# Side work of a half step between its logits and its maxima, on three engines, in a four-layer convolution and attention kernel

## The chip, the cores and the metric

The kernel runs on one NeuronCore of one Trainium2 chip. It is written with an explicit instruction order for each engine and with semaphores between them: TensorE (PE) multiplies, VectorE (DVE) reduces and combines, ScalarE (ACT) evaluates functions, GpSimd (POOL) does three tiny operations an image, and SyncE issues the DMAs. The metric is device time in microseconds.

## The reference, cut to what matters

The input is x, 16 images of 256 channels by 32 by 32, fp32. Four layers follow each other:

```
L0: Q,K,V = 1x1 conv of x to 128 channels; per channel a 32x32 attention:
    attn = softmax(Q K^T), y = attn V; x = batchnorm(conv(y)) + x
L1: xn = group_norm(x, 32 groups); q,k,v of 8 heads, 32 channels each, t = 1024 positions
    logits = (q*s)^T (k*s)              (1024 x 1024 for each head and image)
    weight = softmax(logits); out = w_proj (v weight^T) + b; x = x + out
L2: xn = group_norm(x, 16 groups); k,v = kv_w xn + b
    q = softmax(k over channels)*s; k = softmax(k over positions)
    out = gelu(group_norm((k v^T)^T q)); x = xn + out_w out + b
L3: add bias; upsample by 2 (12 taps, both axes); leaky ReLU * sqrt 2; downsample by 2
```

Inputs and outputs are fp32; nothing is computed on the host beyond laying out weights.

## The kernel before

The attention of L1 is the main stream. An image has 32 steps: two groups of four heads, two halves of the 512 query positions, and eight tiles of 128 key positions (STEPS = UNITS * NT). A step has two half steps, called pairs in the code, one for each two of the four heads. So an image has 64 half steps, numbered 2 * n + pair, and the period of one image b is a loop over them. In a half step the engines do:

- L, logits (line 1097): TensorE multiplies two heads' keys and queries into PSUM banks 0 and 1, and ScalarE takes their exponentials, E (line 944), into prob. The next logits into a bank wait for the exponential two before.
- M, maxima (max_products, line 1112): TensorE computes, for the step ten steps ahead (m = n + NT + LEAD), two products of 128 queries by 512 keys into the three banks 2, 3, 5 in turn. VectorE takes their row maximum, R (max_steps, line 659), and ScalarE the exponential less that maximum with its sum over the row, U (sums, line 956), so that softmax's row factors are known before the weights are computed. Product k waits for the sum k - 3: the second product of a half step therefore waits for the first sum of the half step before.
- V, values (line 1141): only in the half step with pair 0, that is the even ones. TensorE multiplies the weights of the step before with v, for four heads, into bank 4.
- S, side work: a list of small named tasks of all other layers. The table SIDE (line 53) gives each half step its names. A name can stand for work of TensorE, ScalarE, VectorE, SyncE and GpSimd at once, each engine walking the same table in its own program. Names of image b finish its own L1 projections (q1, k1, v1), of image i = b - 1 they do the projection, L2 and L3 (proj, kv, qT, o2, z, wu, hu, hd, wd), and of image j = b + 1 they do L0 and the start of L1 (l0, corr, av, wr, q0, k0, v0). Side products use PSUM banks 6 and 7; bank_free (line 1155) gives for each name the wait that frees its bank. "turn1" to "turn4" pass row factors of softmax between VectorE and TensorE.

TensorE has no side work in the half steps 0, 4, 10, 20, 23, 24, 26 and 43. In 18, 30, 32 and 36 it is short. Names used further on: q1a to k1b are halves of projections which ScalarE evicts (hi, line 991) and VectorE finishes (lo, line 648); v1a and v1b follow in 6 and 7; kv0 to kv7 are evicted by two additions of VectorE (lines 719, 720); proj0a to proj1b by line 710; wr0a to wr1b by line 640; qT0a to qT1b by a copy (line 771); corr0 and corr1 (line 1636) are 64 small products each in half step 21, followed by softmax work on VectorE and ScalarE (soft0a, soft0b, ksub0, ksub1, soft1, qe1, kexp0, kexp1), and ctx0a, ctx0b (line 1701) in 22 need kexp0 and kexp1; norm1a, norm2a, norm3a average statistics (line 1094). In L3, wu and hu (lines 1733, 1743) are the upsampling products, evicted by a VectorE transpose (line 789) and by ScalarE's Prelu into u (line 1027); hd and wd (lines 1751, 1760) downsample, evicted by transposes (lines 797, 804).

The order inside a half step before the change is:

```
TensorE: L  M  V(even)  S
ScalarE: E  U  S
VectorE: R  (normalise, every 16th)  S
```

SyncE and GpSimd walk the table alone. Before the first period, first() does the side work that image 0 needs and its first ten steps of maxima; after the last one, last(i) does the remaining names of image 15 in the order TAIL.

Of the kernel before, what the change touches and what calls it, by code (L numbers as in the profile page):

```python
# [107 lines left out]
def beside(n, i, j):  # L108

    for name in SIDE.get(n, ()):  # L110
        if name == "copy_x" or name.startswith(OF_B) or (i is not None and not name.startswith(OF_J)) \
                or (j is not None and name.startswith(OF_J)):
            yield name
# [17 lines left out]
def chain_kernel(nc, x, weights, vectors, rows, filters, consts, recd, out):  # L131
    with ExitStack() as ctx:
# [223 lines left out]
        def turn_at(n):  # L356


            return (n - 1) // NT + 1 if n % NT == NT - LEAD else None
# [142 lines left out]
        def _(dve):  # L502
# [156 lines left out]
            def max_steps(b, m, pair):  # L659

                k = 4 * (2 * (m % 2) + pair) + m % NT // 2
                for e in range(2):
                    at = Q4 * m + 2 * pair + e
                    dve.wait_ge(max_mm.sem, max_mm(b, at + 1))
                    dve.tensor_reduce(mxh[:, k, e:e + 1], ps[:, max_bank(b, at), :], AX_X, ALU.max,  # L665
                                      negate=True).then_inc(max_ok.sem, 1)
# [244 lines left out]
            def period(b, i, j):  # L911
                for n in range(STEPS):
                    t = turn_at(n)
                    if t is not None:
                        if t < UNITS or j is not None:
                            maxima_joined(b, t)
                    for pair in range(2):
                        m = n + NT + LEAD
                        if m < STEPS:
                            max_steps(b, m, pair)  # L920
                        elif j is not None:
                            max_steps(j, m - STEPS, pair)

                        of, u = (b, n // NT - 1) if n else (i, UNITS - 1)
                        if n % NT == 0 and pair == 0 and of is not None:
                            normalise(of, u)
                        for name in beside(2 * n + pair, i, j):
                            side(name, b, i, j)

            def last(i):  # L930
                normalise(i, UNITS - 1)
                for name in TAIL:
                    side(name, None, i, None)

            periods(first, period, last)

        @block.scalar
        def _(act):
# [27 lines left out]
            def halves(b, t):  # L966

                act.wait_ge(join_v.sem, join_v(b, 2 * t + 2))
                act.activation(apart[:, :, :], apart[:, :, :], ACT.Exp).then_inc(apart_ok.sem, 1)
# [82 lines left out]
            def period(b, i, j):  # L1052
                for n in range(STEPS):
                    for pair in range(2):
                        exponentials(b, i, n, pair)
                        t = turn_at(n)
                        if t is not None and pair == 0 and (t < UNITS or j is not None):
                            halves(b, t)
                        m = n + NT + LEAD
                        if m < STEPS:  # L1060
                            sums(b, m, pair)
                        elif j is not None:
                            sums(j, m - STEPS, pair)
                        for name in beside(2 * n + pair, i, j):
                            side(name, b, i, j)

            def last(i):
                for name in TAIL:
# [5 lines left out]
        def _(pe):  # L1074
# [22 lines left out]
            def logits(b, n, pair, i):  # L1097

                u, s = n // NT, n % NT
                for h in (2 * pair, 2 * pair + 1):  # L1100
                    k = Q4 * n + h

                    if k >= 2:
                        pe.wait_ge(p_ok.sem, p_ok(b, k - 1))
                    elif i is not None:
                        pe.wait_ge(p_ok.sem, p_ok(i, STEPS * Q4 + k - 1))
                    if s == 0 and h == 0:
                        pe.wait_ge(row_in.sem, row_in(b, u + 1))
                    pe.matmul(ps[:, k % 2, :], ks[0:STACK + 1, (u // 2) * Q4 + h, s * P:(s + 1) * P],  # L1109
                              qs[0:STACK + 1, u, h, :], start=True, stop=True).then_inc(s_mm.sem, 1)  # L1110
# [724 lines left out]
            def period(b, i, j):  # L1835
                for n in range(STEPS):
                    for pair in range(2):
                        logits(b, n, pair, i)
                        m = n + NT + LEAD
                        if m < STEPS:  # L1840
                            max_products(b, m, pair)
                        elif j is not None:
                            max_products(j, m - STEPS, pair, b)
                        if pair == 0 and (n or i is not None):
                            of, before = (b, n - 1) if n else (i, STEPS - 1)
                            values(of, before, i)
                        for name in beside(2 * n + pair, i, j):
                            side(name, b, i, j)

            def last(i):  # L1850
                values(i, STEPS - 1)
# [69 lines left out]
```

## Time and profile before

| | |
|---|---|
| median of three runs | 3770.84 us (3764.8 to 3772.77) |
| the profiled execution's own time | 3771.88 us |
| its span, first to last instruction | 3769.7 us |
| TensorE busy | 3572.7 us, 95% |
| ScalarE busy | 2968.4 us, 79% |
| VectorE busy | 2739.3 us, 73% |
| mean granted TensorE clock | 0.971 |

All times are of one execution taken by the hardware profiler. A row of the timeline gives a start and a duration in us, the engine, the line of the kernel, the operation with what it writes and reads, and how many such instructions are merged (x2); in brackets stands the time that the engine sat idle before and what ended it. An fp32 matrix product appears as two MATMUL instructions. Matmuls overlap in the records, so that starts tell more than durations. Image 7 lies from 1649.21 to 1872.21 us, and image 6 ends where it begins.

### The profile page before, as it was taken

How to read it: one execution, taken by the hardware profiler on the slowest of the kernel's cores; microseconds unless marked ns; L12 is line 12 of the kernel's file. 1: busy time of each engine (PE TensorE's matmuls, PEld its weight loads, DVE VectorE, ACT ScalarE, POOL GpSimd, SP SyncE). 2: the span in 40 equal slices, each digit the busy share in tenths (PEclk: the TensorE clock that was granted, in tenths of full speed). 3: DMA queues.
4: the chain of work that ended last, by engine and by line, in shares of the span. 5: the costliest groups of instructions: out<-in, count | busy, mean ns of one | idle time of the engine just before them, and what ended most of it. 6: DMA issues, size and time to landing. Idle time of an engine off the chain costs nothing.

```text
span 3769.7 us, 60230 instructions
## 1 busy us (share of the span) xinstructions
PE 3572.7 (95%) x22401; PEld 1773.8 (47%) x22401; DVE 2739.3 (73%) x4891; ACT 2968.4 (79%) x6992; POOL 41.4 (1%) x57
## 2 busy tenths in 40 slices
PE   6999999999999999999999999999999999999987
PEld 3445545354453545545354454545545354454423
DVE  5667778677777877778677787867778677787645
ACT  2888888888788887888878788887878878788852
POOL 0000000000000000000000000000000000000000
PEclk7889999999999999999999999999999999999998
DMA  2212120121211112120121211112120121211000
GB/s 78 60 40 63 41 71 7 51 60 40 73 38 37 44 43 68 40 71 12 48 58 46 68 38 46 34 44 67 41 72 13 48 56 46 68 38 48 21 17 12
DMA packets 75523, 175.79 MB, mean 47 GB/s; under 512 B 16352, under 2 KB 19040, under 8 KB 73184
## 3 DMA queue, kind: packets, MB, share of 16 engines
q1 hardware_dynamic: 74512, 170.69, 16.6%
q8 instruction: 178, 2.92, 0.3%
q10 hardware_dynamic: 720, 1.26, 0.1%
q14 instruction: 113, 0.93, 0.1%
HBM read 36.62 MB, written 17.30 MB: 14 GB/s over the span
## 4 chain that ended last, share of the span: by engine, by line
PE 80%; ACT 10%; DVE 6%; issue 3%; DMA 0%; SPq 0%; ACTq 0%; POOL 0%; DVEq 0%; POOLq 0%
PE ps L1081 30%; PE ps L1150 12%; PE ps L1109 11%; PE ps L1129 10%; ACT ps L963 5%; PE ps L1701 3%; PE ps L1751 3%; ACT u L1027 2%; ACT prob L954 2%; PE ps L1733 2%; PE ps L1636 2%; PE ps L1648 2%; PE ps L1760 2%; DVE mxh L665 1%; PE ps L1743 1%
## 5 line engine op out<-in xcount | busy, mean ns | idle before, releaser
L665 DVE TENSOR_REDUCE mxh<-ps 128x1 f32<-128x512 f32 x2048 | 1306.9, 679 | 297.9 <-PE ps L1129 291.4
L963 ACT ACTIVATE ps<-ps,mxh 128x512 f32<-128x512 f32 x2048 | 1371.1, 679 | 155.0 <-DVE mxh L665 132.4
L954 ACT ACTIVATE prob<-ps 128x512 f32<-128x512 f32 x2048 | 1124.7, 613 | 316.9 <-PE ps L1109 309.8
L1109 PE MATMUL ps<-qs,ks 97*128 97x512 f32 x2048 | 880.7, 507 | 10.6 <-ACT prob L954 10.5
L1129 PE MATMUL ps<-ks,qs 96*128 96x512 f32 x2048 | 690.6, 413 | 23.9 <-ACT ps L963 15.7
L1109 PEld LDWEIGHTS ps<-qs,ks 97*128 97x128 f32 x2048 | 348.6, 192 | 560.2 <-issue 297.5
L1150 PE MATMUL ps<-prob,vo 128*32 128x512 f32 x4096 | 566.2, 626 | 0.2 <-ACT prob L954 0.2
L1129 PEld LDWEIGHTS ps<-ks,qs 96*128 96x128 f32 x2048 | 396.1, 194 | 166.2 <-ACT ps L963 61.5
L963 ACT ACTIVATION_READ_ACCUMULATOR ps<-ps,mxh 128x1 f32 x2048 | 454.3, 222 | 0.0
L1081 PE MATMUL ps<-xn,wqk 128*128 128x512 f32 x512 | 246.2, 614 | 13.3 <-DVE lo L648 9.3
L1081 PE MATMUL ps<-wkv,xn 128*128 128x512 f32 x512 | 245.0, 608 | 3.7 <-DVE xn L592 3.7
L1081 PE MATMUL ps<-xb,wq 128*128 128x512 f32 x384 | 182.4, 606 | 9.1 <-SPq L440 7.5
L648 DVE SCALAR_TENSOR_TENSOR lo<-ps,vec,hi 128x512 fp32r<-128x512 f32 x128 | 95.9, 749 | 129.5 <-ACT hi L991 129.5
L797 DVE STREAM_TRANSPOSE k<-ps 128x512 f32<-128x512 f32 x128 | 133.2, 1079 | 74.5 <-PE ps L1751 74.5
L1743 PE MATMUL ps<-qe,up_m 64*128 64x512 f32 x512 | 143.6, 638 | 33.6 <-DVE qe L789 12.2
L1150 PEld LDWEIGHTS ps<-prob,vo 128*32 128x32 f32 x4096 | 81.8, 109 | 182.6 <-issue 178.9
L991 ACT ACTIVATE hi<-ps,vec 128x512 fp32r<-128x512 f32 x128 | 88.5, 691 | 95.1 <-PE ps L1081 95.0
L1081 PEld LDWEIGHTS ps<-xn,wqk 128*128 128x128 f32 x512 | 93.9, 193 | 142.8 <-issue 121.9
L1751 PE MATMUL ps<-u,dn_m 128*64 128x512 f32 x512 | 130.5, 611 | 28.4 <-ACT u L1027 23.9
L1027 ACT ACTIVATE u<-ps 128x1024 f32<-128x1024 f32 x128 | 134.8, 1056 | 26.8 <-PE ps L1743 26.8
L1081 PEld LDWEIGHTS ps<-wkv,xn 128*128 128x128 f32 x512 | 92.8, 191 | 122.0 <-issue 110.9
L1701 PE MATMUL ps<-v,k 128*128 128x257 f32 x512 | 134.5, 414 | 4.3 <-ACT k L1014 4.3
(120 smaller groups left out, 3434.2 us busy)
## 6 DMA issues: line engine op xcount, KB each, us to landing
qs<-hi SPq DMA_DIRECT2D x256, 128.0 KB, 2.4
ks<-hi SPq DMA_DIRECT2D x252, 128.0 KB, 2.3
xb<-in_x SPq DMA_DIRECT2D x32, 512.0 KB, 4.4
qs<-lo SPq DMA_DIRECT2D x128, 128.0 KB, 2.4
xa<-xb SPq DMA_DIRECT2D x16, 1024.0 KB, 4.7
recs<-recd SPq DMA_DIRECT2D x64, 256.0 KB
out<-xn SPq DMA_DIRECT2D x32, 512.0 KB, 2.6
ks<-lo SPq DMA_DIRECT2D x126, 128.0 KB, 2.3
```

The source lines that it names most:

```text
L665: dve.tensor_reduce(mxh[:, k, e:e + 1], ps[:, max_bank(b, at), :], AX_X, ALU.max, negate=True).then_inc(max_ok.sem, 1)
L797: dve.transpose(d1[:, p, :].rearrange("p (h c) -> p c h", h=H)[:, 16 * half:16 * half + 16, :], ps[:, bank_of(f"hd{ct}{half}{'ab'[p]}", i) ...
L954: act.activation(prob[:, n % 2, h, :], ps[:, k % 2, :], ACT.Exp).then_inc(p_ok.sem, 1)
L963: act.activation(ps[:, bank, :], ps[:, bank, :], ACT.Exp, bias=mxh[:, k, e:e + 1], accum_out=sumh[:, m // NT % 2, k, e:e + 1]).then_inc(su ...
L1027: act.activation(u2[:, q // 2, q % 2, :, :].rearrange("p a n -> p (a n)"), both(bank_of(name, i)), ACT.Prelu, alpha=SLOPE).then_inc(u2_in. ...
L1081: ins = pe.matmul(dst, lhsT, rhs, start=(n == 0), stop=(n == len(pairs) - 1))
L1109: pe.matmul(ps[:, k % 2, :], ks[0:STACK + 1, (u // 2) * Q4 + h, s * P:(s + 1) * P], qs[0:STACK + 1, u, h, :], start=True, stop=True).then_ ...
L1129: pe.matmul(ps[:, max_bank(b, k), :], qs[0:STACK, u, head, (s // 2) * P:(s // 2 + 1) * P], ks[0:STACK, (u // 2) * Q4 + head, e * HALF:(e + ...
L1150: ins = pe.matmul(ps[DH * h:DH * h + DH, 4, :], vo[:, s, (u // 2) * Q4 + h, :], prob[:, n % 2, h, :], start=(s == 0), stop=(s == NT - 1))
L1701: ins = pe.matmul(ps[:, bank_of(f"ctx{ct}", i), 0:C + 1], k2[:, t, ct * P:(ct + 1) * P], v2[:, t, :], start=(t == 0), stop=(t == NT - 1))
L1743: ins = pe.matmul(ps[:, bank_of(f"hu{ct}{q}", i) + g, :], up_m[rows, :], u1[rows, q // 2, (q % 2) * HALF:(q % 2 + 1) * HALF], start=True, ...
L1751: ins = pe.matmul(ps[64 * g:64 * g + 64, bank_of(f"hd{ct}{half}{'ab'[p]}", i), :], dn_m[:, :], u2[:, half, p, g, :], start=True, stop=True)
```

## The change

In the period loops of TensorE, ScalarE and VectorE the two lines that run the side work move. TensorE runs S between L and M, ScalarE between E (with the exponentials of `halves`) and U, VectorE ahead of R. SyncE's and GpSimd's programs, the table, the banks, the waits and all instructions stay as they are, as do first() and last().

```
--- before.py
+++ after.py
@@ VectorE, period @@
                     for pair in range(2):
+                        for name in beside(2 * n + pair, i, j):
+                            side(name, b, i, j)
                         m = n + NT + LEAD
                         if m < STEPS:
                             max_steps(b, m, pair)
...
                         if n % NT == 0 and pair == 0 and of is not None:
                             normalise(of, u)
-                        for name in beside(2 * n + pair, i, j):
-                            side(name, b, i, j)
@@ ScalarE, period @@
                             halves(b, t)
+                        for name in beside(2 * n + pair, i, j):
+                            side(name, b, i, j)
                         m = n + NT + LEAD
                         if m < STEPS:
                             sums(b, m, pair)
                         elif j is not None:
                             sums(j, m - STEPS, pair)
-                        for name in beside(2 * n + pair, i, j):
-                            side(name, b, i, j)
@@ TensorE, period @@
                         logits(b, n, pair, i)
+                        for name in beside(2 * n + pair, i, j):
+                            side(name, b, i, j)
                         m = n + NT + LEAD
                         if m < STEPS:
                             max_products(b, m, pair)
...
                             values(of, before, i)
-                        for name in beside(2 * n + pair, i, j):
-                            side(name, b, i, j)
```

## Rows read from the trace of the kernel before

**Rows 1.** The page, part 1: busy us (share) xinstructions of each engine.
```profile
PE 3572.7 (95%) x22401; PEld 1773.8 (47%) x22401; DVE 2739.3 (73%) x4891; ACT 2968.4 (79%) x6992; POOL 41.4 (1%) x57
```

**Rows 2.** Windows: us, PE PEld DVE ACT POOL busy, PEclk, DMA share, GB/s.
```profile
...
1649.21:1872.21 223.00, 216.81 (x1402) 108.81 (x1400) 170.64 (x305) 185.60 (x437) 2.07 (x3) 1.00 0.18 48
72.50:295.00 222.50, 200.48 (x1211) 95.89 (x1209) 145.03 (x252) 190.26 (x486) 0.69 (x1) 0.85 0.19 48
1506.50:1509.80 3.30, 3.30 (x12) 0.93 (x11) 3.27 (x6) 2.30 (x3) 0.00 (x0) 0.50 0.01 2
...
```

**Rows 3.** Waits of TensorE: line, engine waited for: us, times, longest.
```profile
...
PE ps L1751 <- ACT u L1027: 23.9, 30, 1.0
PE ps L1129 <- ACT ps L963: 15.7, 37, 2.3
...
PE ps L1743 <- DVE qe L789: 12.2, 31, 1.7
...
```

**Rows 4.** Timeline: start us, us, instruction; half steps 23, 24, 44 (last row).
```profile
...
1513.59 0.63 PE L1129 MATMUL ps<-ks,qs 96*128 96x512 f32 x2
1514.02 2.13 DVE L665 TENSOR_REDUCE mxh<-ps 128x1 f32<-128x512 f32 x3
...
1514.74 0.66 ACT L963 ACTIVATE ps<-ps,mxh 128x512 f32<-128x512 f32 x1
...
1515.03 0.39 PE L1129 MATMUL ps<-ks,qs 96*128 96x512 f32 x1
...
1515.57 0.50 PE L1129 MATMUL ps<-ks,qs 96*128 96x512 f32 x1 [0.16 <-ACT ps L963]
...
1806.33 1.07 PE L1129 MATMUL ps<-ks,qs 96*128 96x512 f32 x2 [0.47 <-ACT ps L963]
...
```

**Rows 5.** Timeline, half steps 10 and 11 of image 7.
```profile
...
1685.23 1.03 PE L1109 MATMUL ps<-qs,ks 97*128 97x512 f32 x2
...
1686.10 0.63 PE L1129 MATMUL ps<-ks,qs 96*128 96x512 f32 x2
...
1686.17 0.42 DVE L720 TENSOR_TENSOR v<-ps,rowc 128x256 f32<-128x256 f32 x1
...
1686.53 1.29 DVE L665 TENSOR_REDUCE mxh<-ps 128x1 f32<-128x512 f32 x2
...
1686.66 1.06 PE L1150 MATMUL ps<-prob,vo 128*32 128x512 f32 x8
...
1687.65 0.74 PE L1109 MATMUL ps<-qs,ks 97*128 97x512 f32 x2
...
1688.23 0.63 PE L1129 MATMUL ps<-ks,qs 96*128 96x512 f32 x2
...
```

**Rows 6.** Timeline, starts of half steps 0, 4 and 6 of image 7.
```profile
...
1649.21 0.74 PE L1109 MATMUL ps<-qs,ks 97*128 97x512 f32 x2
1649.32 1.25 DVE L804 STREAM_TRANSPOSE xn<-ps 128x1024 f32<-128x1024 f32 x1 [1.04 <-PE ps L1760]
...
1663.64 1.03 PE L1109 MATMUL ps<-qs,ks 97*128 97x512 f32 x2
...
1664.25 0.75 DVE L710 SCALAR_TENSOR_TENSOR xa<-ps,vec,xa 128x512 f32<-128x512 f32 x1 [0.97 <-PE ps L1081]
...
1671.87 1.03 PE L1109 MATMUL ps<-qs,ks 97*128 97x512 f32 x2
...
1673.20 0.75 DVE L648 SCALAR_TENSOR_TENSOR lo<-ps,vec,hi 128x512 fp32r<-128x512 f32 x1 [0.28 <-ACT hi L991]
...
```

**Rows 7.** Timeline of FIR work, half steps 47 to 49 of image 7.
```profile
...
1817.33 0.73 PE L1109 MATMUL ps<-qs,ks 97*128 97x512 f32 x2
...
1818.84 1.13 PE L1743 MATMUL ps<-qe,up_m 64*128 64x512 f32 x4 [0.32 <-DVE qe L789]
...
1820.64 1.02 ACT L1027 ACTIVATE u<-ps 128x1024 f32<-128x1024 f32 x1
...
1823.83 1.06 ACT L1027 ACTIVATE u<-ps 128x1024 f32<-128x1024 f32 x1
...
```

More of the change, by code:

```diff
@@ L917, in period @@
                     for pair in range(2):
+                        for name in beside(2 * n + pair, i, j):
+                            side(name, b, i, j)
                         m = n + NT + LEAD
@@ L926, in period @@
                             normalise(of, u)
-                        for name in beside(2 * n + pair, i, j):
-                            side(name, b, i, j)
             def last(i):
@@ L1058, in period @@
                             halves(b, t)
+                        for name in beside(2 * n + pair, i, j):
+                            side(name, b, i, j)
                         m = n + NT + LEAD
@@ L1063, in period @@
                             sums(j, m - STEPS, pair)
-                        for name in beside(2 * n + pair, i, j):
-                            side(name, b, i, j)
             def last(i):
@@ L1838, in period @@
                         logits(b, n, pair, i)
+                        for name in beside(2 * n + pair, i, j):
+                            side(name, b, i, j)
                         m = n + NT + LEAD
@@ L1846, in period @@
                             values(of, before, i)
-                        for name in beside(2 * n + pair, i, j):
-                            side(name, b, i, j)
             def last(i):
```

## The prediction, made before the changed kernel ran

> **What bounds the kernel now.** I read the busy line of the page first, then the windows over one whole image, the waits of TensorE, and last the timeline of the half steps that the change touches. TensorE is busy for 3572.7 us of 3769.7 [rows 1]. One steady image (the 223.0 us from the first logits of one image to those of the next) has 216.8 us of TensorE, 185.6 of ScalarE and 170.6 of VectorE [rows 2]. So TensorE is the engine that sets the pace of 14 of the 16 images, with 6.2 us of visible idle each, and the other two have 37 and 52 us of slack. That idle stands where late side work waits on side work: the FIR products wait for ScalarE's u (23.9 us in all) and for VectorE's qe (12.2); waits for ScalarE's sums are only 15.7 us over the run [rows 3]. Such slack is an average, though. The question is whether each TensorE instruction still finds its input ready, since everything behind a waiting one stands still.
>
> **The loop that matters.** Maxima of a half step write two of three PSUM banks in turn. The second product of a half step takes the bank that the first sum of the half step before gives back: product, VectorE maximum, ScalarE sum, next product. The loop's length can be read where it already binds: product at 1513.59, maximum 1514.02 (+0.43), sum 1514.74 (+0.72), product 1515.57 (+0.83), 1.98 us together, and the row says that this product waited for the sum [rows 4]. The same wait, 0.47, stands at 1806.33 in half step 44 [rows 4], behind the one odd half step that has an empty side block: the loop shows itself wherever nothing but logits separates two maxima pairs. The +0.43 holds only if VectorE is free. If VectorE still has side work for d us after TensorE's part of it ended, the loop is d + 1.55.
>
> On TensorE's side a maxima pair takes 0.56 (1686.10 to 1686.66), four values 0.99 (1686.66 to 1687.65), a logits pair 0.58 (1687.65 to 1688.23), and two products follow 0.24 apart (0.63 for two against 0.39 for one) [rows 4, 5]. From the first product of one half step to the second of the next that is 0.56 + 0.58 + 0.24 = 1.38, plus what else is issued between them. (After an fp32 side product the logits pair is recorded 0.29 early, 1.03 long against 0.74 [rows 5]; I take that off where I count from it.)
>
> **The change, part by part.** No instruction is added or removed, and DMA and GpSimd orders stay; the three engines place each side block S after the logits L instead of behind maxima M and values V. V exists in even half steps only, right behind M. TensorE's order was L M V S and is L S M V. Two things follow. Between the maxima of two half steps stood the first one's block; now the second one's stands there (with V, when the second is odd, in both orders). Between the blocks of two half steps stood L and M of the second, with V if that is even; now M of the first, with V if that is even, and L: going into an odd half step the distance grows from 1.14 to 2.13, going into an even one it shrinks from 2.13 to 1.14. Also VectorE's maximum, formerly ahead of its own half step's side work, now stands behind it, and ScalarE's sums likewise. I walked one image, half step by half step (numbers 0 to 63, the keys of SIDE), with durations of the trace. Wait at the second product = d + 1.55 - 1.38 - S, less 0.99 when the half step is odd.
>
> 1. Even half steps without TensorE side work: 0, 4, 10, 20, 26. The odd block before each stood between the two maxima pairs; now only a logits pair does. Take 10: the kv1 block ends at about 1685.52 (1685.23 + 0.29), VectorE's two additions end at 1686.53, so d = 1.0 [rows 5] and the wait is 1.0 + 0.17 = 1.2. Half step 0: VectorE's result transpose lasts from 1649.32 to 1650.57 against a block that ended at 1649.21: d about 1.3, wait 1.45. Half step 4: the last residual (1664.25 + 0.75) against 1663.93: d 1.05, wait 1.2 [rows 6]. 20 and 26 have no VectorE tail: 1.98 - 1.38 = 0.6 each. Sum 5.05.
> 2. Even half steps with a short block (18, 30, 32, 36: transposes and averages of 0.2 to 0.5 us). The tail is an eviction of 128x512 near 0.75 plus its start delay [rows 6], d about 0.95: 0.6 each at 30 and 32, 0.35 at 36, 0.85 at 18, where kmaxS also waits for ScalarE's l0kb. Sum 2.4.
> 3. Side blocks that depend on the block before, going into an even half step, now 1.14 us behind instead of 2.13. v1a at 6 needs the bank that the low part of k1b frees: that eviction ends at 1673.95, 1.79 after its block's true end (1671.87 + 0.29) [rows 6], against 1.14 plus a small average: 0.45. The second maxima of 2 behind q1a's low part: 0.45. wr1b and o20b at 34 behind VectorE's statistics: 0.75. Sum 1.65.
> 4. Half steps 21 to 25. Before, maxima and values cover the time in which ScalarE finishes kexp1 for ctx0b. Now the 5.4 us of corr0 and corr1 are followed by M21 and L22 alone, and U21, E22 and U22 come later on ScalarE, so the logits of 24 wait more than now. Net +0.5, bounds 0 to 1.3.
> 5. Half steps 38 to 44: the average norm3a loses its wait of 0.5 (it goes into an odd half step), z0a gains 0.7 behind the gelu, 42 gains, and the wait at the maxima of 44 goes while turn3 waits for VectorE's join. Net -0.2, bounds -1.5 to +1.
> 6. FIR, 45 to 63. Here ScalarE already sets the pace: ScalarE's u of hu00 and hu01 start 3.19 us apart (1820.64, 1823.83) [rows 7]. The same E, U and u work in another order has the same pace. The waits going into odd half steps shrink (hu00's 0.32 [rows 7]) and come back going into even ones: wu01 0.37 and wu11 0.37 for the transpose before them (it lets the next product go 1.51 after the block, 1817.33 to 1818.84), M52 0.4. Net +1.0, bounds -4.7 (every wait of this stretch gone) to +3.5 (ScalarE's blocks at their full recorded lengths, 3.5 a half step).
>
> Sum of one image: 5.05 + 2.4 + 1.65 + 0.5 - 0.2 + 1.0 = 10.4 us. Items 1 and 2 take ScalarE and VectorE as free when the loop asks for them; if the delays they cause give later half steps room, half of the sum may be hidden (low 5); added to the high ends of 4 to 6 it is 15. Fourteen images: 146 us. The first image has no work of an image before it, so most half steps have no block and their order does not change: +3 (0 to 8). The last has no maxima from half step 44 on: +6 (2 to 10). The part before the first logits of image 0 and the tail of the last are not touched. 155 us on the profiled execution's own 3771.88 gives 3927; that execution is 1.0 above the median of the three runs, so 3926 is predicted.
>
> A rule beside this: the Trainium skill (Perfetto Trace Analysis, Identifying the Most-Contended Engine) says that matmul busy time is no good measure of how near TensorE is to its limit, and wants weight-load busy time instead. Weight loads are 108.8 us of the 223.0 here [rows 2]; by that TensorE would have half its time free and rival C below would be likelier. The trace is against it: in rows 5 each group of products starts as the one before it has passed, without a wait named, and that is what the sum rests on.
>
> **The rivals.**
> A, faster: the waits that vanish are worth more than those that appear. Blocks in odd half steps get 0.99 more distance, and such blocks (hu, hd, norm) hold most recorded waits. An image has 6.2 us of idle [rows 2], some 1.1 of it on sums (15.7 over 14 images [rows 3]); if the other 5.1 all go and nothing comes back, 14 x 5.1 = 71, so 3700. It decides if the loop of three banks is no longer than 1.38, so that the second product finds its sum also in an empty even half step. Against it: rows 4 show the loop at 1.98.
> B, more than forecast: added waits let TensorE's clock fall. The granted clock is 0.50 (1.2 GHz, the lower of the two levels) from 1506.50 to 1509.80, right after the small products of corr [rows 2], while TensorE still counts as busy; image 0, with TensorE busy for 200.5 of 222.5 us (90%), runs at 0.85 [rows 2]. At 92 to 93% busy, each further image that loses two such stretches loses 3.3 us more, half of 6.6: 14 x 3.3 = 46, so 3972. The skill (TensorE: Matmul & The Clock Gate, Part 1) has the low clock as the default that activity releases; that makes this likelier, and the row of 1506.50 agrees in that weak activity, not idleness, precedes the fall.
> C, half or less: ScalarE's and VectorE's slack (37 and 52 us an image) takes the delays: 5 us an image, 70 + 9, 3849; at the extreme no change, 3771.
> D, the blocks move but the loop never binds because each even half step's maxima were late anyway: same as no change, 3771.
>
> **How the numbers follow.** Forecast (3880 to 3950) 0.50; B and the high bounds (over 3950) 0.16; C at half (3780 to 3880) 0.20; C or D at nothing (within 0.2%, some 8 us, which is about what a measurement of this kernel can tell from no change) 0.04; A 0.10. Range 3810 to 3985: it leaves out A, no change and the far end of B. Faster 0.10, same 0.04, slower 0.86.
>
> **What would show it.** In the new trace: TensorE's waits at the maxima line for ScalarE's sums go from 15.7 us to over 80, five to nine an image, each about 0.6 to 1.4 us and in even half steps; TensorE's busy share in a steady image falls from 97% to 93%; waits of norm3a vanish; ScalarE's idle time before the sums, waiting for the maximum, grows. The prediction is wrong if an image still takes 226 us or less, if half step 10 shows no wait at its second product, or if the added time stands at another place (logits waiting for exponentials, say).

## The result: 6% slower, and the profile after

The changed kernel takes 3995.38 us (median of four runs, 3989.9 to 3997.59) against 3767.82 (3764.17 to 3772.77) for the kernel before on the same chip: ratio 1.060, 95% interval 1.058 to 1.062. The direction and the main mechanism were as predicted; the loss is 1.47 times the forecast (227.6 us against 155), and the time lies 10 us above the range.

The page of the changed kernel: its span, the busy times (those of before are [rows 1]), the 40 slices of the clock, the chain of waits by engine, and the group of ScalarE's sums.

```profile
span 3995.3 us, 60228 instructions
...
PE 3696.1 (93%) x22401; PEld 1785.6 (45%) x22401; DVE 2733.4 (68%) x4891; ACT 2936.2 (73%) x6992; POOL 41.3 (1%) x57
...
PEclk7889999999999999999999999999999999999998
...
PE 62%; ACT 20%; DVE 14%; issue 4%; DMA 0%; ACTq 0%; SPq 0%; POOL 0%; DVEq 0%; POOLq 0%
...
L963 ACT ACTIVATE ps<-ps,mxh 128x512 f32<-128x512 f32 x2048 | 1363.3, 673 | 708.6 <-DVE mxh L665 704.3
```

ScalarE and VectorE have not become slower; both are a little less busy than before. What changed is who waits: the sums' idle time for the maximum was 132.4 us and is 704.3, and the chain that sets the end now runs through ScalarE and VectorE for a third of its length (34%, before it was 16%). TensorE's waits (line, engine waited for: us, times, longest), of which [rows 3] gave those of before:

```profile
PE ps L1129 <- ACT ps L963: 110.5, 138, 3.0
PE ps L1109 <- ACT prob L954: 40.0, 63, 0.7
PE ps L1743 <- ACT u L1027: 18.8, 45, 0.5
...
PE ps L1081 <- DVE vo L654: 11.8, 14, 0.9
```

The same view of the kernel before has these for the logits and for hu (its longest row for u at L1751, 23.9, is in [rows 3] and is 4.7 now):

```profile
PE ps L1109 <- ACT prob L954: 10.5, 17, 1.0
PE ps L1743 <- ACT u L1027: 9.9, 15, 0.7
```

Waits for sums went from 15.7 us to 110.5, eight to nine an image; the waits of the logits for their exponentials from 10.5 to 40.0. Of the 138 waits for sums 131 stand in even half steps, and in nearly every image at 0, 4, 10, 20, 26, 30, 32 and 36. The waits of the logits stand at 24, 42 and 44, 0.66 us each.

Half step 10 of image 7, to be laid beside [rows 5] (start us, us, instruction, in brackets the idle time before):

```profile
1787.73 1.03 PE L1129 MATMUL ps<-ks,qs 96*128 96x512 f32 x2
...
1788.33 0.42 DVE L719 TENSOR_TENSOR k<-ps,rowc 128x256 f32<-128x256 f32 x1 [1.89 <-PE ps L1081]
...
1788.60 0.63 PE L1109 MATMUL ps<-qs,ks 97*128 97x512 f32 x2
1788.67 0.42 DVE L720 TENSOR_TENSOR v<-ps,rowc 128x256 f32<-128x256 f32 x1
...
1789.01 1.88 DVE L665 TENSOR_REDUCE mxh<-ps 128x1 f32<-128x512 f32 x3
1789.07 0.40 PE L1129 MATMUL ps<-ks,qs 96*128 96x512 f32 x1
1789.72 0.66 ACT L963 ACTIVATE ps<-ps,mxh 128x512 f32<-128x512 f32 x1 [1.42 <-DVE mxh L665]
...
1790.55 0.49 PE L1129 MATMUL ps<-ks,qs 96*128 96x512 f32 x1 [1.08 <-ACT ps L963]
...
1790.97 1.07 PE L1150 MATMUL ps<-prob,vo 128*32 128x512 f32 x8
1791.06 1.08 ACT L954 ACTIVATE prob<-ps 128x512 f32<-128x512 f32 x2
```

This is the forecast's loop, step by step. VectorE's maximum stands behind the two additions of half step 9 (1789.01, as d = 1.0 had it), the sum follows 0.71 later, the next product 0.83 after that. First and second product start 1.48 apart and not 0.24: 1.24 of delay, where the forecast has 1.2. Of it the wait list counts 1.08: the first product passes through alone, which is recorded as busy (0.40 and 0.49 against 0.63 for a pair). So a list of waits alone undercounts the loss, by 0.16 here. The split pairs are also a part of why TensorE's busy time grows by 123 us with the same 22401 instructions: about 0.26 for each of 201 split pairs (138 waits for sums, 63 for exponentials) is some 52 us, an estimate. The rest is mostly a matter of how products behind fp32 work are recorded, and neither work nor waiting (the busy time of the maxima products grows by 238 us, that of the logits falls by 106): the pair behind an fp32 side product is recorded early and long, and that is now the maxima pair (1.03 in the first row here, 0.63 in [rows 5]) where it was the logits pair (0.63 here, 1.03 there).

The last row shows a second loop: the exponentials of half step 10, whose logits started at 1788.60, run at 1791.06, because on ScalarE they stand behind the two sums that waited for the maximum. At half step 10 nothing waits for them; at 24, 42 and 44 the logits do. Of these the forecast priced only 24 (its item 4).

The first image and a steady one, windows of the changed kernel (us, PE PEld DVE ACT POOL busy, PEclk, DMA share, GB/s; steady before: [rows 2]):

```profile
103.20:308.00 204.80, 182.66 (x1160) 87.98 (x1158) 118.11 (x206) 162.28 (x404) 0.69 (x1) 0.85 0.18 47
1746.80:1986.20 239.40, 226.63 (x1402) 109.49 (x1401) 170.31 (x306) 183.40 (x437) 2.07 (x3) 0.99 0.17 45
```

and the first image of the kernel before, from the first logits to those of image 1:

```profile
103.20:292.80 189.60, 173.65 (x1160) 83.82 (x1158) 118.67 (x206) 162.14 (x404) 0.69 (x1) 0.90 0.19 50
```

Image by image, from the starts of the logits: +15.2 us in image 0, +198.6 in images 1 to 14 (14.2 each), +11.8 in the last: 225.6, the whole difference of the profiled executions (3997.41 and 3771.88).

### The profile page after: what moved, and what is told of

Read it like the earlier page. It is cut to its first block, busy times and chain, and to the rows that moved or that the text cites. A ratio compares the mean times of both kernels' runs of the same rounds, so it can differ in the third digit from the quotient of the medians.

```text
span 3995.3 us, 60228 instructions
## 1 busy us (share of the span) xinstructions
PE 3696.1 (93%) x22401; PEld 1785.6 (45%) x22401; DVE 2733.4 (68%) x4891; ACT 2936.2 (73%) x6992; POOL 41.3 (1%) x57
## 3 DMA queue, kind: packets, MB, share of 16 engines
q1 hardware_dynamic: 74512, 170.69, 15.7%
## 4 chain that ended last, share of the span: by engine, by line
PE 62%; ACT 20%; DVE 14%; issue 4%; DMA 0%; ACTq 0%; SPq 0%; POOL 0%; DVEq 0%; POOLq 0%
PE ps L1081 21%; ACT ps L963 10%; PE ps L1150 10%; PE ps L1109 9%; PE ps L1129 8%; DVE mxh L665 5%; ACT prob L954 4%; PE ps L1701 3%; PE ps L1751 3%; ACT u L1027 2%; PE ps L1733 2%; PE ps L1636 2%; PE ps L1648 2%; PE ps L1760 2%; DVE qe L789 1%
## 5 line engine op out<-in xcount | busy, mean ns | idle before, releaser
L963 ACT ACTIVATE ps<-ps,mxh 128x512 f32<-128x512 f32 x2048 | 1363.3, 673 | 708.6 <-DVE mxh L665 704.3
L1129 PE MATMUL ps<-ks,qs 96*128 96x512 f32 x2048 | 928.6, 520 | 118.4 <-ACT ps L963 110.5
L1109 PE MATMUL ps<-qs,ks 97*128 97x512 f32 x2048 | 774.9, 450 | 40.0 <-ACT prob L954 40.0
L1109 PEld LDWEIGHTS ps<-qs,ks 97*128 97x128 f32 x2048 | 370.7, 193 | 640.7 <-ACT prob L954 500.6
L1129 PEld LDWEIGHTS ps<-ks,qs 96*128 96x128 f32 x2048 | 371.2, 195 | 628.3 <-ACT ps L963 377.3
L963 ACT ACTIVATION_READ_ACCUMULATOR ps<-ps,mxh 128x1 f32 x2048 | 441.7, 216 | 0.0
L719 DVE TENSOR_TENSOR k<-ps,rowc 128x256 f32<-128x256 f32 x128 | 54.3, 424 | 167.3 <-PE ps L1081 167.3
L1743 PE MATMUL ps<-qe,up_m 64*128 64x512 f32 x512 | 143.6, 639 | 26.6 <-ACT u L1027 18.8
L1081 PE MATMUL ps<-qe,wo 128*128 128x512 f32 x256 | 126.7, 620 | 19.4 <-DVE vo L654 11.8
```

The source lines that it names most:

```text
L963: act.activation(ps[:, bank, :], ps[:, bank, :], ACT.Exp, bias=mxh[:, k, e:e + 1], accum_out=sumh[:, m // NT % 2, k, e:e + 1]).then_inc(su ...
L1081: ins = pe.matmul(dst, lhsT, rhs, start=(n == 0), stop=(n == len(pairs) - 1))
L1129: pe.matmul(ps[:, max_bank(b, k), :], qs[0:STACK, u, head, (s // 2) * P:(s // 2 + 1) * P], ks[0:STACK, (u // 2) * Q4 + head, e * HALF:(e + ...
L1743: ins = pe.matmul(ps[:, bank_of(f"hu{ct}{q}", i) + g, :], up_m[rows, :], u1[rows, q // 2, (q % 2) * HALF:(q % 2 + 1) * HALF], start=True, ...
```

## The experiments

Ratios are to the kernel before on the same chip, each with its 95% interval. "Image" is the mean duration of images 2 to 13: 225.6 us before, 240.4 after. LATE and EARLY are sets of half steps tested in the three loops alike.

### 1. The odd blocks back behind the maxima

The nine even half steps in which the forecast puts the larger waits (items 1 and 2) each follow an odd block; here those nine blocks return to their old place.

```diff
+LATE = (3, 9, 17, 19, 25, 29, 31, 35, 63)
+  for name in beside(2 * n + pair, i, j) if 2 * n + pair not in LATE else (): side(...)   # ahead of maxima
+  for name in beside(2 * n + pair, i, j) if 2 * n + pair in LATE else (): side(...)       # behind
```

> The changed kernel, but in the nine odd half steps that stand before an empty or short even one (3, 9, 17, 19, 25, 29, 31, 35, 63) all three engines keep the order of before, so that the odd block again separates two maxima pairs. Loop theory (the three-bank loop product, maximum, sum, product of 1.98 us or more meets 1.38 us of TensorE work where the second block is empty): the pairs of half steps 0-1, 4-5, 10-11, 18-20, 26-27, 30-33 and 36-37 lost 10.4 of the 14.8 us an image; most of it comes back, some 0.5 to 1 us an image is lost where two blocks now follow at one logits pair's distance: 3830 to 3870. Rival 1 (the cost is that side blocks wait for each other, or the clock falls): 3950 or more. Rival 2 (ScalarE's exponentials queued behind sums in every half step): 3950 to 3990, as 55 half steps keep the new order.

Measured: 3941.76 us, ratio 1.046 (1.044 to 1.048), image 237.3. The losses at 0, 4, 10, 20, 26, 30, 32 and 36 vanish but for 0.1 (half step 10 takes 2.42 as before, half step 4 too; 18 alone does not), as the theory has it; but the time does not return. 54 us came back where 125 to 165 were expected. Half step 3 alone goes from 6.08 to 8.92, 17 from 3.19 to 3.79, 29 from 3.21 to 4.77. The rows of half steps 2 and 3:

```profile
1730.48 1.38 PE L1134 MATMUL ps<-ks,qs 96*128 96x512 f32 x2
...
1732.79 0.73 PE L1114 MATMUL ps<-qs,ks 97*128 97x512 f32 x2
1732.83 0.71 ACT L994 ACTIVATE hi<-ps,vec 128x512 fp32r<-128x512 f32 x1
...
1733.35 0.39 PE L1134 MATMUL ps<-ks,qs 96*128 96x512 f32 x1
1733.57 0.75 DVE L649 SCALAR_TENSOR_TENSOR lo<-ps,vec,hi 128x512 fp32r<-128x512 f32 x1 [2.47 <-ACT hi L994]
...
1734.95 0.66 ACT L966 ACTIVATE ps<-ps,mxh 128x512 f32<-128x512 f32 x1 [1.42 <-DVE mxh L666]
...
1735.79 0.49 PE L1134 MATMUL ps<-ks,qs 96*128 96x512 f32 x1 [2.04 <-ACT ps L966]
```

At a seam from the new order to the old, the maxima pairs of two half steps again have no block between them, and here the maximum of half step 2 stands behind q1b's two-step eviction (ScalarE's high part, then VectorE's low part, until 1734.3). The wait is 2.04. The same happens behind the blocks of 16 and 28: waits of 0.62 at 17 and 1.25 at 29 in 14 images each. My expectation overlooked that returning a block of an odd half step strips the one after the even block before it.

### 2. Only these nine blocks early

```diff
+EARLY = (3, 9, 17, 19, 25, 29, 31, 35, 63)
+  ... if 2 * n + pair in EARLY   # ahead of maxima; all others behind, as before
```

> The complement: the kernel before, with the new order in those nine odd half steps alone. In an empty even half step after an early odd block nothing but logits separates two maxima pairs. Loop theory: the loss of the pairs, 10.4 us an image, appears almost alone: 3900 to 3940. If the loss needs the new order everywhere (rival 2) it is near 9/64 of the whole: 3800 or less.

Measured: 3995.4 us, ratio 1.060 (1.057 to 1.062), image 241.4, TensorE's waits:

```profile
PE ps L1134 <- ACT ps L966: 134.5, 155, 2.3
```

Nine of 64 half steps cost as much as the whole change, and 55 us more than the upper end of what I expected. Half step 0 loses 1.51, 4 loses 0.96, 10 0.95, 30 0.96, 32 0.95: the place is shown twice over, for these are the half steps that the edit leaves without a block between their maxima and the ones before. The equal total is in part luck, though. This run's granted clock is 0.955, against 0.965 in the changed kernel. In images 5 to 14 half step 26 runs at the lower level, and in most of them 27 too (image 7, us, PE PEld DVE ACT POOL busy, PEclk, DMA share, GB/s), which the same half steps of the changed kernel do not:

```profile
1839.93:1848.08 8.15, 8.15 (x148) 4.89 (x146) 5.41 (x11) 6.30 (x16) 0.00 (x0) 0.50 0.01 3
```

Span times what the clock lacked of full speed is 180 us here (0.045 of 4000.2), 140 in the changed kernel and 109 before. So about 160 of the 230 us between the spans are not clock, which is 10 an image, as expected; in the changed kernel it is about 195 of 225 (both are estimates).

### 3. The values between logits and maxima

```diff
@@ TensorE, period of the changed kernel @@
+                        if pair == 0 and (n or i is not None): values(of, before, i)
                         max_products(...)
-                        if pair == 0 and (n or i is not None): values(of, before, i)
```

> The changed kernel with TensorE's values issued ahead of the maxima in even half steps (logits, side, values, maxima). VectorE's and ScalarE's orders stay. Loop theory: the 0.99 us of values now stands between the odd maxima and the even ones, where the waits are, and is gone between even and odd, where blocks are mostly 1 us or longer: gains some 9 us an image at 0, 4, 10, 18, 20, 26, 30, 32, 36, loses some 3 at the FIR blocks of about 1 us and at 23 and 43: 3880 to 3930. Distances between blocks also go back to those of before. Rival 1 (block distances) gives less than half: 3950 to 3995 with waits of side products for evictions gone or moved; rival 2 no change, 3985 or more.

Measured: 4115.12 us, ratio 1.092 (1.089 to 1.095). A miss: 0.99 more distance for the even half steps does shorten the waits for sums, but the logits now wait for exponentials at a quarter of the half steps, and the granted clock falls to 0.948 (214 us short of full speed in 4112.7, against 109 before):

```profile
PE ps L1109 <- ACT prob L954: 118.1, 262, 0.7
PE ps L1129 <- ACT ps L963: 35.5, 58, 2.0
```

With the values ahead of them the maxima stand directly before the next logits, so maxima, maximum, sum, exponential and the logits after next follow each other with nothing in between. This is the second loop of half step 10 above, and it makes common (262 waits) what the changed kernel shows 63 times in the whole run. That the clock's part is a consequence of these waits is not shown.

### 4. Image 0 in the old order

```diff
+  for name in beside(2 * n + pair, i, j) if b > 0 else (): side(name, b, i, j)   # ahead
+  for name in beside(2 * n + pair, i, j) if not (b > 0) else (): side(name, b, i, j)   # behind
```

> The changed kernel with the order of before in the period of image 0 alone. Image 0 took 15.2 us more than before where I had said 3. If that excess belongs to its own period's order (the loop, on an image in which ScalarE was thought to set the pace), this gives 15 us back: 3980. If it is carried in from clock phases or the start, it stays at 3995.

Measured: 3976.24 us, ratio 1.055 (1.053 to 1.058). Image 0 takes 185.0 us instead of 204.8, and its window shows the clock as well:

```profile
103.20:288.20 185.00, 169.74 (x1159) 82.16 (x1158) 117.70 (x205) 161.32 (x403) 0.69 (x1) 0.93 0.20 52
```

TensorE's waits for sums inside image 0, in the changed kernel and then in the kernel before:

```profile
PE ps L1129 <- ACT ps L963: 11.8, 15, 2.0
PE ps L1129 <- ACT ps L963: 4.1, 6, 2.3
```

So the new order adds 7.7 us of these waits to image 0, and the granted clock goes from 0.90 to 0.85. Length times what the clock lacked of full speed is 19 us before (189.6 us), 31 in the changed kernel (204.8 us) and 13 here (185.0 us). The two parts overlap: together they are more than the 15.2 us of difference, so they do not split it. The four runs of experiments 4 to 7, whose image 0 has the order of before, take 184.5 to 186.4 us in it against 189.5 in the profiled execution before; the 15.2 us of image 0 are therefore rather a low figure than a high one.

### 5 to 7. The one empty half step of the kernel before

If the loop of three banks is what binds, it can be relieved in the kernel before as well: half step 43 has no block, and 44 waits [rows 4]. Moving z0b's block from 42 to 43 puts work there. The bank rotation also restarts with each image (128 products, not a multiple of 3), and that happens at half step 44; going on in turn frees the bank one product earlier.

```diff
 # 5
-42: ["z0b"], 44:
+43: ["z0b"], 44:
 # 6
-... else MAX_BANKS[k % 3]
+... else MAX_BANKS[(k + b * STEPS * Q4) % 3]
-pe.wait_ge(sum_ok.sem, sum_ok(i, STEPS * Q4 - (1, 0, 2)[k]))
+pe.wait_ge(sum_ok.sem, sum_ok(i, STEPS * Q4 + k - 2))
 # 7: both
```

> The kernel before with one name moved: z0b from half step 42 to the empty half step 43. In the order of before, 43 is the only odd half step with an empty block, so its maxima and those of 44 are separated by logits alone, and the trace of before shows TensorE waiting there for ScalarE's sums (0.47 in the timeline of image 7, and again at the second product). Loop theory: with 1.65 us of products in that gap the wait goes, 1.0 to 1.3 us an image in 15 images: 3750 to 3757 against 3770. Rival (the wait is ScalarE's backlog behind the gelu's table loads, whatever lies in the gap): no change, 3768 to 3772.

> The kernel before, with the rotation of the three maxima banks carried on from image to image. 128 products do not divide by three, so at the change of image (half step 44) the first product waits for the first sum of 43 and the second for the second; carried on, the first waits for the second sum of 42 and the second for the first of 43, as everywhere else. Loop theory: the wait at 44 shrinks by one sum's time, 0.67: 3758 to 3763. Rival (ScalarE's backlog): no change.

> Both. With z0b in the gap neither bank is waited for, so the rotation adds little: within 3 us of the kernel with z0b moved alone, 3748 to 3757. Rival: no change against before.

Measured: 3752.95 us, ratio 0.9948 (0.9931 to 0.9964); 3751.9, 0.9953 (0.9941 to 0.9966); 3752.15, 0.9949 (0.9937 to 0.9961). The wait for sums at 44 (0.46 in 15 images) is gone in 5 and 0.16 in 6, each by another way, and together they give nothing more, as one shared cause requires. These are versions with an unchanged result that beat both kernels, by 0.5%: little, but the intervals leave out 1. (5: half step 42 is 1.42 shorter, 43 is 1.06 longer and 44 is 0.47 shorter, so 0.83 us less an image. 6: half step 44 is 0.59 shorter. Times 15 images that is 9 to 12 of the 15 to 16 us; where the rest comes from was not followed.) They are also the change's opposite in small: a block put where there was none.

### 8. Only the FIR stretch early

```diff
+  ... if 2 * n + pair > 44   # ahead of maxima; the rest behind, as before
```

> The new order in half steps 45 to 63 alone (FIR), that of before elsewhere. In the changed kernel these half steps took 1.8 us more an image; alone they should show the same and the wait of half step 0 (d of the last transpose, 1.45 to 1.8) does go with them, as block 63 is then ahead of its maxima and half step 0 late: 1.8 + 1.7 an image, 3770 + 50: 3810 to 3830. If the FIR loss in the changed kernel is backlog carried in from 38 to 44, the stretch alone costs under 0.5 and the sum is under 3800.

Measured: 3842.04 us, ratio 1.020 (1.018 to 1.022), 5.35 us an image, 12 us above the upper end of what I expected. Half steps 46 to 63 are as long as in the changed kernel (+2.0 together as recorded), half step 0, behind the early block of 63, loses 1.90, and 44 and 45, at the seam, 0.68. So the FIR stretch makes its loss itself and does not inherit it, and it is not the place where most of the change's cost arises.

### 9 and 10. A maximum over half the columns

Both take the maximum over 256 of the 512 columns (the other half is left out of the maximum; the products and sums stay whole). It shortens the loop and leaves TensorE's work as it is.

```diff
-ps[:, max_bank(b, at), :], AX_X, ALU.max,
+ps[:, max_bank(b, at), 0:HALF // 2], AX_X, ALU.max,
```

> The changed kernel with VectorE's maxima taken over 256 of the 512 columns (part of the maximum is left out, so the output differs), which shortens VectorE's part of the loop from 0.65 to about 0.4 an instruction. Loop theory: each of the waits behind it (some 15 an image) shrinks by 0.25 to 0.5: 5 to 7 us an image: 3890 to 3930. Rival (side evictions, logits behind exponentials or the clock carry the loss): 3970 or more.

> The same in the kernel before, as the yardstick: the loop binds in one place an image there, so 3760 to 3770. If VectorE's work as such sets the pace in both kernels, both gain alike.

Measured: in the changed kernel 3900.88 us, ratio 1.035 (1.032 to 1.037), 94 us less; in the kernel before 3738.15, 0.9925 (0.9898 to 0.9953), 30 us less. In the changed one the products of half steps 0, 4, 10, 20, 32 and 36 start 0.26 closer to each other; where the loop does not bind (half steps 5, 11, 14) the durations stay. The kernel before gains a third of that, more than I expected (0 to 10 us), at 44 (0.52) and in spots of the FIR stretch. So some 64 of the 94 us belong to the changed order.

```profile
PE ps L1129 <- ACT ps L963: 79.3, 134, 2.8
PE ps L1109 <- ACT prob L954: 37.3, 64, 0.7
```

The number of waits hardly falls (134 against 138), their length does (31 us in all). The granted clock is 0.972 here against 0.965, which is another 31 us of the 94 (109 us short of full speed against 140).

### 11. The gelu's neighbourhood in the old order

```diff
+LATE = (40, 41)
```

> The changed kernel, but half steps 40 and 41 keep the old order on all three engines. In the changed kernel half step 41 is 1.69 us longer than before: ScalarE's gelu (2.37 us and a table load on either side) stands ahead of the sums of 40, and TensorE issues z0a, which needs the gelu, right behind the logits. Theory (a queue of in-order work behind the gelu): sums of 40 go ahead of the gelu and M41 and V stand ahead of z0a, so half step 41 gives back 1.3 to 1.7 us; but the seam from 39 to 40 (maxima of 40 directly behind its logits, blocks of 39 on VectorE unfinished) costs 0.5 to 1.0 of it. Net -0.3 to -1.0 us an image, 3980 to 3991 us. Rival (the 1.69 us are only time moved in from the half steps around it, since 38 to 44 together cost 0.7): 41 gives back 1.7, and 40 and 44 take it all; 3993 to 3997 us.

Measured: 4027.94 us, ratio 1.070 (1.068 to 1.072): neither theory. Half step 41 does return to 4.83 us exactly, 1.69 less, but half step 40 goes from 5.65 to 9.19:

```profile
1914.20 0.75 DVE L649 SCALAR_TENSOR_TENSOR lo<-ps,vec,hi 128x512 fp32r<-128x512 f32 x1 [1.93 <-ACT hi L994]
...
1915.59 0.66 ACT L966 ACTIVATE ps<-ps,mxh 128x512 f32<-128x512 f32 x1 [1.42 <-DVE mxh L666]
...
1916.41 0.50 PE L1134 MATMUL ps<-ks,qs 96*128 96x512 f32 x1 [2.04 <-ACT ps L966]
...
1916.85 1.58 PE L1155 MATMUL ps<-prob,vo 128*32 128x512 f32 x8
...
1918.36 3.11 PE L1086 MATMUL ps<-xn,wqk 128*128 128x512 f32 x4
```

It is the seam of experiment 1 again: k0a's block in 39 ends in a high and a low part, so the wait is 2.04 and not the 0.5 to 1.0 that I gave it. The values (1.58 instead of 1.06) and k0b's products (3.11 for four, against 1.88 to 1.96 elsewhere) behind it are longer too, and the granted clock is 0.63 from 1916.85 to 1921.50. Shown twice, then: behind a block with a two-step eviction the recorded wait is about 2.0 us; behind a one-step one (half step 10) it is 1.1.

### 12. TensorE in the old order, ScalarE and VectorE in the new

```diff
@@ TensorE, period of the changed kernel @@
-                        for name in beside(2 * n + pair, i, j): side(name, b, i, j)
                         max_products(...)
                         values(...)
+                        for name in beside(2 * n + pair, i, j): side(name, b, i, j)
```

> TensorE in the order of before (logits, maxima, values, side work), ScalarE and VectorE in the changed order (side work ahead of sums and maxima). It asks what the agreement of the three orders is worth. Theory: the maximum and the sum of a half step now stand behind evictions of side products that TensorE issues after the maxima products and the values, so the second product of the next half step, 0.82 us behind the end of the block (logits 0.58, 0.24), waits for d + 1.5: with d near 1.0 that is about 1.5 us in each of some 50 half steps with a block, 60 to 80 us an image: 4600 to 4950 us, and TensorE's waits for sums are over 700 us. Rival (only TensorE's order matters, ScalarE and VectorE have slack of 37 and 52 us an image to take the delay): 3772 to 3850 us.

Measured: 5687.75 us, ratio 1.509 (1.506 to 1.512), an image about 353 us. One half step (9) of image 7, and the waits:

```profile
2516.70 0.40 PE L1129 MATMUL ps<-ks,qs 96*128 96x512 f32 x1
2516.77 0.41 DVE L720 TENSOR_TENSOR v<-ps,rowc 128x256 f32<-128x256 f32 x1
2517.10 1.28 DVE L665 TENSOR_REDUCE mxh<-ps 128x1 f32<-128x512 f32 x2
2517.82 0.66 ACT L963 ACTIVATE ps<-ps,mxh 128x512 f32<-128x512 f32 x1 [3.24 <-DVE mxh L665]
...
2518.65 0.50 PE L1129 MATMUL ps<-ks,qs 96*128 96x512 f32 x1 [1.55 <-ACT ps L963]
```

```profile
PE ps L1129 <- ACT ps L963: 1192.3, 852, 5.0
```

The wait of one half step was right (1.5 expected, 1.55 measured), and the count, 50 to 55 an image, too. The total is 740 us above the upper end of my range: the span is 5676.8 us at a granted clock of 0.854. Of the 1907 us between the spans 1177 are recorded waits for sums, and the clock is up to 720 more: 829 us short of full speed (0.146 of 5676.8) against 109 before (0.029 of 3769.7). The price of a wait counted by its recorded length is far too low when there are many of them. It also shows what the change keeps right: the three orders agree, and this disagreement costs eight times the loss of the change. The opposite one, TensorE in the new order and the other two in the old, was not run.

## Why the prediction was right in kind and some 70 us short

**In short.** The loop was read rightly, and the sum made from it was too small. Of the 71 us that are missing, 53 are in images 1 to 14 (198.6 against 146), 12 in image 0 (15.2 against 3) and 6 in the last (11.8 against 6). The step that failed is the adding up: it priced the loop at nine half steps of a middle image, put the clock at nothing, gave image 0 hardly any new wait, and priced too low what late sums do behind the gelu and in the FIR stretch.

**What held.** The bound, the loop and its three durations, and the distance on TensorE. Of the signs named in advance, waits for sums over 80 us are there (110.5), so are five to nine an image (138 in 16), above all in even half steps; TensorE's busy share in a steady image falls from 97% to 95% (93% forecast, too low because busy time grew as well, as half step 10 shows); ScalarE's idle time before the sums grew fivefold. Experiments 1, 2, 9 and 12 show the loop as the cause at the nine half steps, which are 8.9 of the 14.8 us an image: moving blocks moves the waits, and shortening the maximum shortens them. For the rest of the loss the loop is argued from the rows. Rival A is refuted: although the waits for u at L1751 did fall from 23.9 to 4.7 and those for qe from 12.2 to 1.7, some 30 us in all, over 130 came for them (94.8 for sums, 29.5 for exponentials, 8.9 for u at L1743). C is refuted too: ScalarE and VectorE had the slack, but in the wrong places. D as well. B, the clock, was no rival but a part of the loss.

**The sum of one image, term by term** (means over images 2 to 13; a logits pair behind an fp32 product is recorded 0.29 early, as the prediction says, and this is taken off or added where the change moves such a product):

```
                              forecast  measured
1 empty even half steps          5.05      5.9    (0: 1.8, 4: 1.2, 10: 1.2, 20: 0.8, 26: 0.8)
2 short even ones                2.4       3.0    (18: 0.7, 30: 0.8, 32: 0.8, 36: 0.6)
3 dependent blocks               1.65      0.7    (2: 0.2, 6: 0.5, 34: 0.0)
4 half steps 21 to 25            0.5       0.9
5 half steps 38 to 44           -0.2       0.7
6 FIR, 45 to 63                  1.0       2.1
not in the sum: all others        0        1.5    (half step 1: 0.5; the rest 0.22 each or less)
sum                             10.4      14.8    (14.2 over images 1 to 14)
```

The forecast gave one image bounds of 5 to 15 us, and 14.2 lies inside them; 15.2 for image 0 and 11.8 for the last lie outside theirs (0 to 8, 2 to 10).

**The steps that failed, one by one.**

- The clock stood among the rivals (B) and not in the sum. Mean granted clock times span gives 109 us short of full speed before (0.029 of 3769.7) and 140 after (0.035 of 3995.3): at most 31 of the 71 us. By stretches the trace has some 12 of them in image 0, 12 in images 1 to 14 and 5 in the last. The place is different from what B had, and B's window for image 0 (72.50 to 295, at 0.85) began 31 us ahead of that image's first logits; the image itself ran at 0.90. In image 7 the fall comes behind the wait of half step 0 (windows of the changed kernel; the second is the same half step of image 6, without a fall):

```profile
1746.80:1751.40 4.60, 3.24 (x13) 0.76 (x11) 3.24 (x5) 3.21 (x9) 0.00 (x0) 0.76 0.28 114
1508.30:1511.94 3.64, 2.28 (x14) 0.71 (x12) 3.24 (x5) 2.26 (x6) 0.00 (x0) 1.00 0.35 144
```

The mean of 0.76 is a mixture of 1.00 (2.4 GHz) and 0.50 (1.2 GHz), and the engine stood idle for the same 1.36 us of recorded wait in both. In six of the 16 images the trace has the lower level in half step 0, and in four in half step 24; before it was two and none. In 21 or 22, behind the small products of corr, nearly every image has it in both kernels. The Trainium skill (TensorE: Matmul & The Clock Gate, Part 1) has the throttled clock as the default, which activity releases. Image 7, with its fall behind an added wait, agrees; that the same wait brings no fall in image 6 is explained by no run here.
- Image 0: "most half steps have no block and their order does not change: +3". The premise holds and the conclusion does not. An empty half step behind an early block is the very place where the loop binds, and image 0 has more such places than a middle image: its waits for sums go from 6 to 15 and from 4.1 to 11.8 us, for example 2.02 at half step 3, behind the two-step eviction of q1b, 1.02 at 8, behind v1b, and 1.08 at 32. With them its clock falls from 0.90 to 0.85 (experiment 4).
- "The last: +6". It has all of items 1 to 5, so 9.4 by the forecast's own terms; it lost 11.8. It too has empty half steps of its own, since the names of a next image are missing. The longest wait for a sum of the whole run, 3.02, stands in one of them: in half step 16 TensorE has no l0ka, and the maximum of 15 (3734.28) stands on VectorE behind kmax0's reduction (1.90 from 3732.47).
- Item 5. The norm3a wait vanished as forecast (half step 39 is 0.57 shorter), the one for sums at 44 too (0.67), though the logits of 44 now wait 0.66 for their exponentials in all 16 images (43 is 0.53 longer). And z0a behind the gelu was priced at 0.7 and costs 1.69. In the rows the sum of half step 40 starts at 1909.43, behind gelu and a table load, the exponentials of 41 at 1910.77, and then the logits of 42 wait 0.66:

```profile
1905.75 2.37 ACT L1022 ACTIVATE qe<-qe,gb,ga 128x1024 f32<-128x1024 f32 x2
...
1908.14 1.28 ACT L963 ACT_TABLE_LOAD   x1
...
1908.27 1.95 PE L1081 MATMUL ps<-qe,wo 128*128 128x512 f32 x4 [0.84 <-DVE vo L654]
...
1909.43 0.66 ACT L963 ACTIVATE ps<-ps,mxh 128x512 f32<-128x512 f32 x1
...
1910.77 1.08 ACT L954 ACTIVATE prob<-ps 128x512 f32<-128x512 f32 x2
...
1911.42 0.99 PE L1109 MATMUL ps<-qs,ks 97*128 97x512 f32 x2 [0.66 <-ACT prob L954]
```

- Behind item 5 lies one thing that the prediction walked past: E of a half step stands behind U of the one before, so a sum that comes late makes the exponentials late as well. Waits of the logits for exponentials rose by 29.5 us, about 2 an image, nearly all of it at 24, 42 and 44. I had it as a sign that would refute the forecast ("logits waiting for exponentials"); it is in fact the same loop, one turn further, and it is less than a third of what the waits for sums grew by.
- Item 6, FIR: 1.0 forecast, 2.1 measured. Experiment 8 shows that the stretch makes its loss itself; which of its waits it is was not taken apart.

**What stays open.** How the clock's 31 us divide between waits for sums and for exponentials, and why one wait is followed by the lower clock and another not; how the new order of each engine by itself contributes, since only one of the mixed orders was run; and some 0.1 us in each of a dozen half steps, for which no experiment was made. Item 3 was too high by 0.9 (half step 34 lost nothing), which was not followed up.

## What to carry to other kernels

Where engines hand a few buffers round in a loop (product, maximum, sum, the bank back), first write down the loop's length and the distance that the order leaves it on the engine that sets the pace, for each place, not on average: 1.98 us and more against 1.38 made most of a 6% loss here although both helpers were idle for 37 and 52 us an image. Independent work is worth most between two turns of the loop, and an order that alternates long and empty blocks should have each empty one stand beside a long one; look for places where the list has no entry at all, since filling the one of the kernel before gave 0.5%. Then count such places in the first and the last turn of the outer loop as well, where part of the list is missing. And an added wait costs its recorded length, 0.16 us for the broken pair (half step 10), sometimes everything that its helper engines issue in order after it, and sometimes the clock.

## What was unexpected of the hardware

- TensorE's busy time can rise without more work. A pair of products split by a wait is recorded as 0.40 and 0.49 us, against 0.63 together. And a pair behind an fp32 product is recorded as 1.03, so the mean of the maxima products rises from 413 to 520 ns while that of the logits falls from 507 to 450, with the same shapes: they changed places behind the side work.
- The granted clock of a whole run goes with the waits only roughly: 0.971 with 15.7 us of waits for sums, 0.965 with 110.5 and 0.854 with 1192.3, but 0.955 with 134.5 (experiment 2) and 0.972 with 79.3 (experiment 9).
- The same wait of 1.36 us at half step 0 is followed by the lower clock in some images and not in others (0.76 and 1.00 in the windows above).
